# A decoder kernel on one core: attention's moment sums as 64x64 tiles in paired units, integer turns and the norms' last step on ScalarE

## The reference, cut to what matters

```python
def _layernorm(x, axis=-1, eps=1e-05):
    m = jnp.mean(x, axis=axis, keepdims=True)
    v = jnp.var(x, axis=axis, keepdims=True)
    return (x - m) / jnp.sqrt(v + eps)

# attention ("a"): K = 32 heads, H = 8 channels a head, M = 4 angles
z = causal_depthwise_conv(x @ in_proj_w, conv_w, taps=4) + conv_b   # 256 + 256 + 32 columns
x_val, x_gate, s_raw = z[..., :D], silu(z[..., D:2 * D]), z[..., -K:]
p_w = exp(clip(score_scale * s_raw, -20, 20)) * time_weight         # per head
phi = x_val[..., None] * theta                                      # (b, l, K, H, M)
poly = w[0] + w[1] * x5 - w[2] * square(x5)
num_re, num_im, den = cumsum([p_w * poly * cos(phi), p_w * poly * sin(phi), p_w], axis=1)
re, im = num_re / max(den, 1e-4), num_im / max(den, 1e-4)
rs = rsqrt((sum(re ** 2) + sum(im ** 2)) / (2 * H * M) + 1e-5)      # over a head's H * M moments
y = re * rs * norm_scale[:H * M] @ W_re + im * rs * norm_scale[H * M:] @ W_im   # 32 -> 8 per head
attn = (y * x_gate) @ out_proj_w

# cross attention ("b"): autocorrelation by DFT, the best 5 lags per head, weighted rolls of V
# feed forward ("c"): 8 experts x 64, two branches: prod = xV * cumsum(yW), router softmax, U, W_O
x = _layernorm(x + attn(x)); x = _layernorm(x + xattn(x, ctx)); x = _layernorm(x + ffn(x))
```

## Time and profile before

| | |
|---|---|
| Median of 3 runs | 1076.63 us (1075.76 to 1078.91) |
| The profiled execution | 1077.53 us |
| its span, first to last instruction | 1075.7 us |
| PE busy | 960.7 us (89%) |
| DVE busy | 852.4 us (79%) |
| ACT busy | 471.9 us (44%) |
| POOL busy | 45.9 us (4%) |
| mean granted clock of TensorE | 0.963 of full speed |

### The profile page before, as it was taken

The page is one execution under the profiler, slowest core; times in us unless marked ns, Lnnn a source line. Parts: engine busy times, 40 slices in busy tenths (PEclk is TensorE's granted clock), DMA queues, the critical chain, the costliest instruction groups (busy, mean ns, idle before and its releaser), DMA issues. The chain is left out here.

```text
span 1075.7 us, 10422 instructions
## 1 busy us (share of the span) xinstructions
PE 960.7 (89%) x3460; PEld 587.8 (55%) x3482; DVE 852.4 (79%) x1459; ACT 471.9 (44%) x736; POOL 45.9 (4%) x64
## 2 busy tenths in 40 slices
PE   2596685889999999999999999999999998998696
PEld 1253352655467545855485547754675467547245
DVE  3769699999997999799989999799979984173232
ACT  1465364268333943285328633583339411410310
POOL 0001000020001000100000000000010001000000
PEclk9799897899999999999999999999999999999789
DMA  7700010010001000010001000100010000000000
GB/s 211 164 1 0 20 39 1 20 39 1 0 21 41 19 1 21 1 59 0 20 1 59 1 0 21 59 1 1 1 52 8 1 1 20 1 0 1 19 1 20
DMA packets 38167, 25.45 MB, mean 24 GB/s; under 512 B 17991, under 2 KB 37474, under 8 KB 38114
## 3 DMA queue, kind: packets, MB, share of 16 engines
q1 hardware_dynamic: 38114, 24.78, 8.0%
HBM read 20.58 MB, written 4.19 MB: 23 GB/s over the span
## 5 line engine op out<-in xcount | busy, mean ns | idle before, releaser
L1462 DVE TENSOR_TENSOR_SCAN sc<-mask,sc 128x1024 f32<-128x1024 bf16 x64 | 146.2, 2284 | 0.1
L585 PE MATMUL ps<-sc,wy 128*128 128x512 f32 x256 | 126.2, 621 | 13.5 <-DVE sc L1462 10.8
L767 PE MATMUL ps<-x2t,mv 128*128 128x512 f32 x256 | 122.5, 601 | 3.2 <-DVE prod L1707 3.1
L758 PE MATMUL ps<-cum,mw 128*128 128x512 f32 x256 | 123.6, 606 | 1.2 <-ACT wparts L1136 1.2
L786 PE MATMUL ps<-up,prod 128*128 128x256 f32 x512 | 115.9, 379 | 0.9 <-DVE prod L1707 0.9
L786 PEld LDWEIGHTS ps<-up,prod 128*128 128x128 f32 x512 | 94.8, 190 | 13.8 <-issue 1.7
L1145 ACT ACTIVATE cs<-ps 128x512 f32<-128x512 f32 x64 | 37.7, 589 | 113.3 <-PE ps L758 112.5
L1454 DVE TENSOR_TENSOR sc<-sc,g 128x1024 f32<-128x1024 f32 x64 | 77.6, 1212 | 9.7 <-ACT sc L1030 9.5
L585 PEld LDWEIGHTS ps<-sc,wy 128*128 128x128 f32 x256 | 48.0, 195 | 66.0 <-issue 50.2
L758 PEld LDWEIGHTS ps<-cum,mw 128*128 128x128 f32 x256 | 47.5, 192 | 60.1 <-issue 59.7
L1375 DVE SCALAR_TENSOR_TENSOR zc<-ps,cw,zc 128x510 f32<-128x510 f32 (+2 forms) x96 | 71.0, 745 | 11.2 <-ACT zc L971 8.9
(11 more groups left out here) (253 smaller groups left out, 1628.3 us busy)
## 6 DMA issues: line engine op xcount, KB each, us to landing
xa<-in_x_dram SPq DMA_DIRECT2D x8, 512.0 KB, 3.9
xs_a<-in_x_dram SPq DMA_DIRECT2D x8, 512.0 KB, 3.8
cin<-in_ctx_dram SPq DMA_DIRECT2D x8, 512.0 KB, 5.6
out_dram<-prod SPq DMA_DIRECT2D x8, 512.0 KB, 4.8
win<-in_L_attn_in_proj_w_dram SPq DMA_DIRECT2D x1, 512.0 KB, 4.1
prod<-in_L_ffn_V_fwd_dram SPq DMA_DIRECT2D x2, 256.0 KB
prod<-in_L_ffn_W_fwd_dram SPq DMA_DIRECT2D x2, 256.0 KB
prod<-in_L_ffn_W_inv_exp_dram SPq DMA_DIRECT2D x2, 256.0 KB
```

Source lines behind the costliest of these rows:

```text
L585: last = mm(y, wy[:, 1 - c, m, :], sc[:, u % 4, c, :], start=(m == 0 and c == 0), stop=(m == M - 1 and c == 1))
L758: last = mm(o, mw[:, t, br, c:c + P], cum[:, t, :], start=(t == 0), stop=(t == 1))
L767: last = mm(o, mv[:, t, br, c:c + P], x2t[:, t, :], start=(t == 0), stop=(t == 1))
L1462: V.tensor_tensor_scan(flat, mask[:, 0:2 * T], flat, 0.0, ALU.mult, ALU.add)\
```

## The change

It has four parts.

1. **Tiles.** The channels of the two value tiles are laid out in other halves: tile 0 holds channels 0 to 63 and 192 to 255, tile 1 holds 64 to 191 (loads of `win`, `cw`, `cb`, `thn` in pieces; `hsel`, `headm`, `psel`/`pouter` follow). `wy` has 64 columns. A product of 128x128 becomes two of 64x64 on the halves r of the partitions. For tile h, half r goes from partitions 64r to output half r XOR h of bank ("Y", r). The two tiles together thus use the four quarters of the array. The Y banks come out in natural channel order.
2. **Pairs.** A unit is now u = 2m + h, and `a_sums(m)` takes units 2m and 2m + 1 together: 8 products (re/im x tile x half), four calls a chunk instead of eight. It waits for both scans, and needs both Y banks at m = 0.
3. **ScalarE.** The whole turns come from ACT (`a_turns`: Identity with a scale per partition, written as int32), and so does the norms' last step (Identity with scale rstd and bias -mean * rstd). POOL has four instructions instead of two, since it makes the bias too.
4. **Order.** All lists are new, and PE, ACT have five stages in flight and NCHUNK + 4 turns. The turns of two units ahead are kept in the two slots of `kturn` as before.

```diff
 def turn ... PE, before
-                c_spread(d, 3) ... a_sums(b, 6) ... a_squares(b) ... a_transpose(a, 0) ... a_out(b, 1)
-                b_out(c, 0) ... b_out(c, 1) c_out(d, 0) c_out(d, 1) b_transform(b, "cf", 0) ...
-                c_transpose(c, 0) c_transpose(c, 1) b_transform(b, "xf", 0) ... c_hidden(c, 0) ... a_sums(a, 0)
...
+            def turn(a, b, c, d, e):
+                c_turn(e)
+                a_spread(b, 0)
+                b_spectrum(d, "qa")
...
+                c_running(e, 3)
+                c_spread(e, 3)
+                a_sums(b, 0)
...
+                b_back(d, 1)
+                a_sums(b, 1)
+                c_out(e, 0)
+                c_out(e, 1)
+                b_out(d, 0)
+                b_out(d, 1)
+                b_transform(c, "cf", 0)
+                b_transform(c, "cf", 1)
+                a_sums(b, 2)
+                c_transpose(d, 0)
+                c_transpose(d, 1)
+                a_sums(b, 3)
+                c_hidden(d, 0)
+                a_squares(b)
+                c_hidden(d, 1)
+                b_transform(c, "xf", 0)
+                a_factor(b, 0)
+                c_hidden(d, 2)
+                a_factor(b, 1)
+                a_transpose(a, 0)
+                c_hidden(d, 3)
+                a_transpose(a, 1)
+                a_out(b, 0)
+                a_scores(a)
+                a_out(b, 1)
+                a_project(a, 0)
+                b_transform(c, "xf", 1)
+                a_project(a, 1)
+                c_logits(d)
+                c_running(d, 0)
```

```diff
             @staged
-            def a_sums(i, u):
-                h, m = divmod(u, M)
+            def a_sums(i, m):
                 if m == 0:
-                    free_a(i, "Y", h)
-                y = ps[:, BANK_A[("Y", h)], :]
-                pe.wait_ge(*VEC_A.at(i, "scan", u))
+                    free_a(i, "Y", 0)
+                    free_a(i, "Y", 1)
+                pe.wait_ge(*VEC_A.at(i, "scan", 2 * m))
+                pe.wait_ge(*VEC_A.at(i, "scan", 2 * m + 1))
                 for c in range(2):
-                    last = mm(y, wy[:, 1 - c, m, :], sc[:, u % 4, c, :], start=(m == 0 and c == 0),
-                              stop=(m == M - 1 and c == 1))
-                last.then_inc(*PE_A.tick("y", u))
+                    for h in range(2):
+                        for r in range(2):
+                            src, dst = slice(r * H, (r + 1) * H), slice((r ^ h) * H, ((r ^ h) + 1) * H)
+                            last = mm(ps[dst, BANK_A[("Y", r)], :], wy[src, 1 - c, m, :], sc[src, (2 * m + h) % 4, c, :],
+                                      start=(m == 0 and c == 0), stop=(m == M - 1 and c == 1))
+                last.then_inc(*PE_A.tick("y", m))
...
-                TS(kturn[:, u % 2, :], zc[:, h, :], thn[:, h, m:m + 1], None, ALU.mult)\
-                    .then_inc(*VEC_A.tick("turns", u))
-                dve.wait_ge(*VEC_A.at(i, "turns", u))
+                m, h = divmod(u, 2)
+                dve.wait_ge(*ACT_A.at(i, "turns", u))
...
+            @staged
+            def a_turns(i, u):
+                m, h = divmod(u, 2)
+                if m == 0:
+                    act.wait_ge(*VEC_A.at(i, "tap", h, 0))
+                if u >= 2:
+                    act.wait_ge(*ACT_A.at(i, "cos", u - 2))
+                elif not is_first(i):
+                    act.wait_ge(*ACT_A.at(i - 1, "cos", UNITS - 2 + u))
+                A(kturn[:, u % 2, :], zc[:, h, :], ACT.Identity, scale=thn[:, h, m:m + 1]).then_inc(*ACT_A.tick("turns", u))
...
+            def ln_apply(i, k, xs, dst, OWN, POOL):
+                act.wait_ge(*POOL.at(i, "rstd", 3))
+                for q in range(NQ):
+                    A(dst[:, q, :], xs[:, q, :], ACT.Identity, bias=rs[k][:, 2, q:q + 1], scale=rs[k][:, 1, q:q + 1])\
+                        .then_inc(*OWN.tick("norm", q))
...
-                G.tensor_tensor(rs[k][:, 0, :], mvr[k][:, :, 1], eps_[:, :], ALU.add)\
-                    .then_inc(*OWN.tick("var"))
-                pool.wait_ge(*OWN.at(i, "var"))
-                G.tensor_tensor(rs[k][:, 1, :], rs[k][:, 0, :], half_[:, :], ALU.pow)\
-                    .then_inc(*OWN.tick("rstd"))
+                G.tensor_tensor(rs[k][:, 0, :], mvr[k][:, :, 1], eps_[:, :], ALU.add).then_inc(*OWN.tick("rstd", 0))
+                G.tensor_tensor(rs[k][:, 2, :], mvr[k][:, :, 0], minus[:, :], ALU.mult).then_inc(*OWN.tick("rstd", 1))
+                pool.wait_ge(*OWN.at(i, "rstd", 1))
+                G.tensor_tensor(rs[k][:, 1, :], rs[k][:, 0, :], half_[:, :], ALU.pow).then_inc(*OWN.tick("rstd", 2))
+                pool.wait_ge(*OWN.at(i, "rstd", 2))
+                G.tensor_tensor(rs[k][:, 2, :], rs[k][:, 2, :], rs[k][:, 1, :], ALU.mult).then_inc(*OWN.tick("rstd", 3))
```

More of the change, by code:

```diff
@@ new lines, in turn @@
+                c_running(e, 7)
+                b_back(d, 0)
+                c_spread(e, 7)
+                c_own(e, 7)
+                b_back(d, 1)
+                a_sums(b, 1)
+                if is_first(b):
+                    for k in [*fold_part(2), *fold_part(3)]:
+                        fold(k)
+                c_out(e, 0)
+                c_out(e, 1)
+                b_out(d, 0)
+                b_out(d, 1)
+                if is_first(c):
+                    pe.wait_ge(folded, len(FOLD))
+                    pe.wait_ge(ready, 2)
@@ L900, in _ @@
+                a_project(a, 1)
+                c_logits(d)
+                c_running(d, 0)
+            for t in range(NCHUNK + 4):
+                turn(*chunks(t, 5))
         @block.scalar
@@ L1145, in c_tile, with a_layer @@
                 A(cs[:, j % 2, :], ps[:, BANK_C[("c", j)], :], ACT.Copy).then_inc(*ACT_C.tick("c", j))
-            def turn(a, b, c, d):
+            def ln_apply(i, k, xs, dst, OWN, POOL):
[3 more added lines that the diff above has]
+                        .then_inc(*OWN.tick("norm", q))
+            @staged
+            def a_layer(i):
+                if not is_first(i):
+                    act.wait_ge(*ACT_B.at(i - 1, "norm", NQ - 1))
+                ln_apply(i, 0, xs_a, x1, ACT_A, POOL_A)
@@ new lines, in b_layer, with c_layer, turn @@
+            @staged
+            def b_layer(i):
+                if not is_first(i):
+                    act.wait_ge(*ACT_C.at(i - 1, "norm", NQ - 1))
+                ln_apply(i, 1, x1, x2, ACT_B, POOL_B)
+            @staged
+            def c_layer(i):
+                ln_apply(i, 2, x2, xs_c, ACT_C, POOL_C)
+            def turn(a, b, c, d, e):
+                b_spectrum(d, "qb")
+                a_turns(b, 3)
+                a_project(b, 2)
+                b_spectrum(d, "ka")
+                b_spectrum(d, "kb")
+                c_tile(e, 1)
+                a_project(b, 3)
+                if is_first(b):
+                    for k in fold_part(None):
+                        fold(k)
+                a_gate(b, 0)
+                b_spectrum(d, "va")
+                c_tile(e, 2)
+                b_spectrum(d, "vb")
+                a_gate(b, 1)
+                a_guard(b)
+                c_tile(e, 3)
+                a_angles(b, 2)
+                b_exp(d)
+                a_turns(b, 4)
+                c_tile(e, 4)
+                a_squares(b, 0)
+                if is_first(b):
+                    for k in fold_part(0):
+                        fold(k)
+                a_angles(b, 3)
+                c_tile(e, 5)
+                b_wt(d)
+                a_turns(b, 5)
+                c_tile(e, 6)
+                a_squares(b, 1)
+                if is_first(b):
+                    for k in fold_part(1):
+                        fold(k)
+                c_tile(e, 7)
+                a_angles(b, 4)
+                a_turns(b, 6)
+                a_squares(b, 2)
+                if is_first(b):
+                    for k in fold_part(2):
+                        fold(k)
+                a_angles(b, 5)
+                b_back(d, 0)
+                a_turns(b, 7)
+                a_squares(b, 3)
+                if is_first(b):
+                    for k in fold_part(3):
+                        fold(k)
@@ L1167, in turn @@
                         fold(k)
-                c_tile(d, 4)
-                b_spectrum(c, "vb")
+                b_layer(d)
+                c_transpose(d, 0)
                 a_squares(b, 7)
@@ L1235, in turn @@
-                b_spectrum(b, "ka")
-            for t in range(NCHUNK + 3):
-                turn(*chunks(t, 4))
+                c_weights(d)
+                c_tile(d, 0)
+            for t in range(NCHUNK + 4):
+                turn(*chunks(t, 5))
         @block.gpsimd
```

485 lines of the change are left out of this document (189 added, 296 removed).

## The result

The changed kernel takes 1103.75 us (median of 4 runs, 1103.52 to 1104.34) against 1077.20 for the kernel before on the same chip: a ratio of 1.0247, interval 1.0229 to 1.0264. It is slower, where I had predicted 1050 us and a gain. The profiled execution has a span of 1101.7 us.

The account below looks back on a forecast made before the run. PE was taken to bound the full rounds, busy 111.7 of 114.1 us. Start 23.7, fill 235, four rounds 432.4 and drain 358 sum to a 1049 us span, hence 1050 us; range 1026 to 1078.

Parts of the forecast that it names:

- The sums on PE: A chunk's sums as 64x64 tiles, four at a time: 6.9 us a round instead of 13.8, PE at 105.6.
- only pairs: Rival, chance 0.08: in the sums only two tiles run together, 115 us a round, 1088 us in all.
- no overlap: Rival, chance 0.04: the sums' tiles run one at a time, 13.8 us a round more, near 1190 us.
- waits in order: Rival, chance 0.15: ACT's in-order norms and late squares cost over 6 us a round; sum 1065 to 1080 us.
- Loads, start and drain: Engine loads a round, setup before the first transpose (23.7 us), and last chunk's first transpose to the end (358 us).
- X(0): First transpose of `xa` for the first chunk, 20.2 us before the change, forecast at 23.7 because of extra loads.
- The sentence that puts the sum otherwise: Restated sum: 49 us less PE work, 22 returning as idle PE at both ends and 4 at start and tail.
- The full rounds: Four rounds, fourth to eighth chunk's first transpose: 108.1 us each against 114.1, together 432.4 against 456.4.
- The fill: First to fourth chunk's first transpose: 235 us, bounds 208 to 263, against 281.3 before.
- The first round: First to second chunk's first transpose: 88 us against 92.5, its one-chunk chain kept, less 4.2 of turns.
- The second round: Second to third chunk's first transpose: 66 us (50 to 80) against 85.8; not under 75 would prove the forecast wrong.
- The third round: Third to fourth chunk's first transpose, with attention and cross attention of the first chunk: 81 us (70 to 95).

## Why the prediction was wrong, by its own steps

**The sums on PE: right.** A group takes 1.88 us (predicted 1.85), PE's round 106.05 (105.6); in two of the four rounds, with the granted clock at 0.98, it is 107.4. The rivals "only pairs" (3.5) and "no overlap" (7) are out. So is "waits in order" as I had put it, a round of 112 to 114. "TensorEngine Tiling (Array Packing)", section Key Properties, in the Trainium skill says that tiles execute in parallel; the trace now agrees for row halves too.

**Loads, start and drain: right.** DVE 96.72 (96.3), ACT 68.6 (71; the ninth table load isn't there: eight in this round and 59 in all, as before), X(0) at 24.0 (23.7), the drain 354.6 (358). The drain was costed stage by stage from PE's instructions, and it is where PE is busy: 145.65 of 150.6 us in the window above. Some of its closeness is luck: the last FFN transpose is at 1029.4, 72.3 us before the end, where I had 78, and what comes before it took 2.3 us more than I had. The sentence that puts the sum otherwise is wrong by 4 us: of the 49 us, 22 come back in all, the start and tail among them.

**The full rounds: mis-sized by 2.3 to 2.6 us each.** I had 108.1 us, it is 110.4 in the window above and 110.7 on average, mostly because PE idles 4.35 us and not 2.5. The stall of `c_transpose` is 2.40 us (bounds 0 to 1.5), `cf` waits 0.87. Two transforms and one group of sums do not hide the norm's chain. That step costs 10.4 us in the sum. Putting the norms back on DVE does not recover it (the four rounds take 443.3 us against 442.8). PE then doesn't stop at `c_transpose`, but 2.1 us right behind it, where `c_hidden` needs ACT's copy of the transposes.

**The fill: the step that failed, by 45.4 us.** Three terms of it:

- *The first round, 88 predicted, 106.9 found.* I wrote that it "keeps its chain of one chunk, less the 4.2 of turns". I left out the one-off work that is threaded through that chain: the order of the folds. The changed order lets them start 9.4 us later and puts them behind waits. With the folds ahead and spread the round is 83.2: the runs show 23.7 us of cost there, more than the 18.9 that was missing.
- *The second round, 66 predicted, 77.9 found.* It was not to be over 75, by my own signs of being wrong. I had subtracted an estimate (19 us of cross attention) from the old load and got 50; attention alone loads DVE with 62.4. The trace of the kernel before had the number: the cross attention's instructions take 11.2 us of DVE's 77.15 in that stretch, not 19. DVE's idle time in the chain of one chunk (15.5 us) comes on top; I had allowed 16 over the load. The cut of DVE's load shows that this load sets the round: 19.8 us less load, 13.8 us less time.
- *The third round, 81 predicted, 95.6 found.* DVE is busy 81.5 of it: I had given as the whole round what is only DVE's load. This round was not tested by itself, and two runs speak against DVE's load alone: with 3.5 us more of it (turns on DVE, 85.08) the round is 0.6 us longer, with 2.4 more (norms on DVE, 83.99) it is 1.7 shorter. What the 14 us are in which DVE idles there stays open.

Taken in one: I treated the fill as work that leaves with the stage that moved out of it. But in the first two rounds PE is not the bound; moving its work (and cross attention) later leaves the chain of DVE, ACT and PE of one attention chunk as it was: PE lost 50.8 us of work in the fill and gained 49.9 of idle time. In the drain the moved work costs in full, 37.0 us. Had I taken DVE's loads as they are measured (62.4 and 81.5) and the idle time of the second round of the earlier trace rows (85.8 - 77.15 = 8.7 us) on top, those two rounds would have come to 71 + 90, and the sum to 23.7 + 88 + 161 + 432.4 + 358 = 1063, with the folds, the 10.4 us of the rounds and the rest of DVE's waits still missing.

**What stays open.** Which link sets the 116 us round of the paired four-stage order was not isolated. Nor was the price of well-placed norms on ACT in that order. No run has five stages without pairs, so what the deeper pipeline is worth by itself is known only with them.

## What to carry to other kernels

A pipeline made one stage deeper has to be costed at both ends separately, each by what bounds that end. Here the drain was TensorE's and grew by 36.8 us, as much as its work. The first two rounds of the fill were held by a chain through VectorE, and the fill gave nothing back until the one-off folds stood in the right place; then it gave 23.4 us, and with the 3.4 us of each of the four rounds that only just paid for the drain. One-off work that is threaded through the first round belongs in the sum: its place in the order was worth 22.8 us, more than the whole tiling. And what an edit is worth depends on the order that it stands in: the turns on a less loaded engine, slower as an instruction, were worth 22.1 us in the five-stage order and 1.0 in the paired four-stage one, and the tiles 20.9 and 1.4. Merely pairing the units, which the tiles need, cost 16.6 us in the old order, beside 4.4 at the start.

## What the runs showed that I had not expected

- Tiles of 64x64 that use all four quarters of the array run at once with different moving data: sixteen instructions of 512 columns, 1.88 us, against 1.71 for four of 128x128.
- With PE busy 39.53 of 77.9 us the mean granted clock was 0.72. At 0.84, with spare products, the groups of sums were faster and began no earlier, since PE was not the bound in that stretch.
- ScalarE's write of a scaled 128x512 tile as int32 takes 719 ns, against 708 for the nearest other instruction of that size with one operand per partition (L1045, written as float32), so the conversion costs next to nothing.
